# One program for two attentions and two feed-forward layers: stages joined without barriers

## The reference

```
x = x + attention_a(layernorm(x))    # 16 heads of 8, causal; heads 0 to 2 up-weight a third of the tokens
x = x + ffn(layernorm(x))
x = x + attention_b(layernorm(x))    # 16 heads of 8, rotary embedding of q and k, no mask
x = x + ffn(layernorm(x))            # the same ffn weights

ffn(x): h = silu(lin1(x)) * lin2(x)  # 128 to 512, ternary weights times a scale per output
        h = gelu(h1(h)); h = gelu(h2(h))   # 512 to 512, exact gelu
        return lin3(h)                     # 512 to 128
```

## Time and profile before

| | |
|---|---|
| time, median of 3 runs | 2213.65 us (2210.31 to 2215.91) |
| the profiled execution: time | 2211.82 us |
| its span, first to last instruction | 2210.1 us |
| mean granted clock of TensorE | 0.947 |
| busy: PE, DVE, ACT, POOL | 1950.2 (88%), 1722.8 (78%), 1476.5 (67%), 1093.7 us (49%) |

### The profile page before, as it was taken

How to read it: one execution, slowest core, us unless ns; L and a number is a source line. 1 busy time by engine, 2 the same in 40 slices (tenths; PEclk the granted TensorE clock), 3 DMA queues, 4 the chain that set the end, 5 groups by cost and what they waited for, 6 DMA issues and landing times. The chain is left out here.

```text
span 2210.1 us, 43095 instructions
## 1 busy us (share of the span) xinstructions
PE 1950.2 (88%) x16198; PEld 991.0 (45%) x16198; DVE 1722.8 (78%) x2358; ACT 1476.5 (67%) x2633; POOL 1093.7 (49%) x1550
## 2 busy tenths in 40 slices
PE   3889989998849999993799999999999976999998
PEld 1333333343337778771122222222222224777776
DVE  4878878888448888851899999999998916888883
ACT  1567767777726666660288888888888973666665
POOL 6777777776415555554233343342433002555555
PEclk9999999999969999996599999999999997999999
DMA  7556555654100000004333444334444110000000
GB/s 171 105 114 130 114 115 122 122 116 104 23 12 1 1 1 1 1 1 99 71 66 70 89 89 96 73 70 96 89 92 85 32 19 5 10 15 10 15 14 16
DMA packets 106212, 136.72 MB, mean 62 GB/s; under 512 B 21008, under 2 KB 89872, under 8 KB 99856
## 3 DMA queue, kind: packets, MB, share of 16 engines
q1 hardware_dynamic: 106000, 133.89, 28.9%
HBM read 67.78 MB, written 55.57 MB: 56 GB/s over the span
## 5 line engine op out<-in xcount | busy, mean ns | idle before, releaser
L709 DVE TENSOR_REDUCE b_negmax<-ps_max 128x2 f32<-128x1024 f32 x512 | 593.2, 1217 | 54.5 <-PE ps_max L848 53.7
L814 ACT ACTIVATE b_prob<-ps_score 128x512 f32<-128x512 f32 x1024 | 552.3, 596 | 97.4 <-PE ps_score L830 88.2
L814 ACT ACTIVATE a_prob<-ps_score 128x512 f32<-128x512 f32 x640 | 346.4, 599 | 91.6 <-PE ps_score L830 83.0
L709 DVE TENSOR_REDUCE a_negmax<-ps_max 128x2 f32<-128x256 f32 (+2 forms) x384 | 314.3, 863 | 84.2 <-PE ps_max L865 79.0
L886 PE MATMUL ps_out<-b_prob,b_v_aug 128*9 128x256 f32 x4096 | 316.8, 382 | 21.7 <-ACT b_o_raw L779 20.9
L609 POOL TENSOR_SCALAR_AFFINE_SELECT a_prob<-a_prob 128x256 f32<-128x256 f32 (+1 forms) x448 | 188.1, 439 | 147.0 <-ACT a_prob L814 146.5
L1143 PE MATMUL ps_score<-fa_h,w_hi 128*128 128x512 f32 x1024 | 247.6, 396 | 0.7 <-ACT fa_h2f L1086 0.4
L1143 PE MATMUL ps_score<-fb_h,w_hi 128*128 128x512 f32 x1024 | 247.5, 396 | 0.7 <-ACT fb_h2f L1086 0.4
L848 PE MATMUL ps_max<-stack_k,b_stack_q 48*128 48x512 bf16 x1024 | 214.2, 394 | 29.9 <-DVE b_negmax L709 14.3
L830 PE MATMUL ps_score<-b_stack_q,stack_k 50*128 50x512 bf16 x1024 | 219.3, 389 | 12.7 <-DMA b_stack_q<-b_nm_rows 7.5
L1143 PEld LDWEIGHTS ps_score<-fa_h,w_hi 128*128 128x128 f32 x1024 | 191.8, 189 | 45.7 <-ACT fa_h2f L1086 0.9
(11 more groups left out here) (155 smaller groups left out, 3194.2 us busy)
## 6 DMA issues: line engine op xcount, KB each, us to landing
stack_k<-d_stack SPq DMA_DIRECT2D x64, 384.0 KB, 6.2
d_stack<-a_parts SPq DMA_DIRECT2D x64, 192.0 KB, 2.8
a_stack_q<-d_stack SPq DMA_DIRECT2D x32, 384.0 KB, 5.6
d_stack<-b_parts SPq DMA_DIRECT2D x64, 192.0 KB, 2.8
b_stack_q<-d_stack SPq DMA_DIRECT2D x32, 384.0 KB, 5.6
d_stack<-a_parts SPq DMA_DIRECT2D x64, 128.0 KB, 2.8
d_stack<-b_parts SPq DMA_DIRECT2D x64, 128.0 KB, 2.8
x<-in_x SPq DMA_DIRECT2D x16, 256.0 KB, 6.7
```

The costliest lines, as they stand in the source:

```text
L709: last = dve.tensor_reduce(m["negmax"][:, t, :, p], banks[:, :, at:at + w], AX.X, ALU.max, negate=True)
L814: act.activation(prob(b, i)[:, o], act_bank("score", 2 * i + o), ACT.Exp).then_inc(s["prob"], 1)
```

## The change

All stages stand in one block with one set of buffers (`buffers`; the attention's and the FFN's large ones overlap in SBUF) and one barrier at the end. Each engine runs attention a's steps -1 to 16, then a joint routine for the attention's steps 17 to 19 and the FFN, then attention b from step 1 or 2, and again the joint routine.
- In the joint routine the norm and transposes of FFN batch 0 lie in step 17, its gates behind step 17 and between the blocks of step 18; the output products of batches 14 and 15 lie behind the gates and in the FFN's batch 0, in bank `ps_out`.
- In the last two batches of the first FFN (r = 14 and 15) the rotary attention's batches 0 and 1 are prepared: norms, transposes, q, qr, k, kr, v in bank `ps_misc`, parts, stores and loads, and step 1 with the maxima of batch 0.
- The flag of the weights is made in steps 8 to 10 of the causal attention, with two small DMAs in place of a transpose. PE reads it after step 17 and branches there, once for each FFN; the attention's drain and the rotary preparation stand inside both branches.
- The rotary attention's weights load during the first FFN. Some semaphores are merged (`moments`; `var` and `neg_mean` share one).

```diff
...
+        first = attention(nc, sem, m, a, "a", True, f)
+        second = attention(nc, sem, m, a, "b", False, f)
+        ffn = feed_forward(nc, m, a, out, f)
+        with nc.Block() as block:
+            @block.sync
+            def _(sp):
+                first.parts["sync_begin"](sp, None)
+                for n in range(-1, B + 3):
+                    first.sync(sp, n)
+                second.parts["sync_begin"](sp, first)
+                second.parts["sync_fill"](sp)
+                for n in range(1, B + 3):
+                    second.sync(sp, n)
+                ffn.sync(sp)
...
+            @block.tensor
+            def _(pe):
+                for n in range(-1, B + 1):
+                    first.tensor(pe, n)
+                ffn.tensor(pe, 0, first, second)
+                for n in range(2, B + 1):
+                    second.tensor(pe, n)
+                ffn.tensor(pe, 1, second, None)
+        nc.all_engine_barrier()
+        nc.clear_and_free_semaphores(own)
+        nc.all_engine_barrier()
...
+    EARLY = {"q": 2, "qr": 2, "k": 2, "kr": 2, "v": 1} if rotary else {}
+    LOOP_END = B + 2
...
+        if rotary and i == 0 and b == 1:
+            sp.wait_ge(f["h1"], count(FT, B))
...
+    def sync_fill(sp):
+        store(sp, 0, "stored_q", 0)
+        load(sp, 0, "stack_q", "stored_q", 0)
+        store(sp, 0, "stored_k", 1)
+        load(sp, 0, "stack_k", "stored_k", 1)
+        store(sp, 1, "stored_q", 0)
...
+        if causal and n == FLAG_STEP:
+            sp.wait_ge(f["halved"], 3)
+            sp.dma_start(m["d_flags"].rearrange("(p o) -> p o", o=1), m["flags"][:]).then_inc(f["flag_moved"], 16)
+        if causal and n == FLAG_STEP + 1:
+            sp.wait_ge(f["flag_moved"], 16)
+            sp.dma_start(m["flag_row"][:], m["d_flags"].rearrange("(o p) -> o p", o=1)).then_inc(f["flag_moved"], 16)
...
+    def pool_fill(pool):
+        high(pool, 1, "q", 0)
+        middle_low(pool, 1, 0)
+        add_bias(pool, 0)
+        pool.wait_ge(f["h3_hi"], count(FT, B))
+        ones(pool, range(1, VALUES))
+        norm(pool, 2)
+        negated_max_parts(pool, 0, 0)
+        high(pool, 1, "k", 1)
+        middle_low(pool, 1, 1)
+        add_bias(pool, 1)
+        high(pool, 2, "q", 0)
+        middle_low(pool, 2, 0)
...
+    def pool_layer(pool, l, before, after):
+        first, left = B * l, before.parts
+        norm_rstd(pool, m, s, first)
+        before.pool(pool, B + 1, 0, 6)
+        norm_rstd(pool, m, s, first + 1)
+        before.pool(pool, B + 1, 6)
+        left["weighted"](pool, B - 2)
+        for r in range(B):
+            b = first + r
+            if r + 2 < B:
+                norm_rstd(pool, m, s, b + 2)
+            if after is None or r < B - 2:
+                low(pool, b, 2, range(FT))
+                if r == 0:
+                    left["weighted"](pool, B - 1)
+                low(pool, b, 3, range(FT))
+                if after is not None and r == B - 3:
+                    after.parts["ones"](pool, (0,))
+                    after.parts["widen_bias"](pool)
+                    after.parts["norm"](pool, 0)
+                continue
+            fill = after.parts
+            if r == B - 2:
+                low(pool, b, 2, range(FT))
+                fill["high"](pool, 0, "q", 0)
+                low(pool, b, 3, range(0, 2))
+                fill["middle_low"](pool, 0, 0)
+                low(pool, b, 3, range(2, 4))
+                fill["high"](pool, 0, "k", 1)
+                fill["middle_low"](pool, 0, 1)
+            if r == B - 1:
+                low(pool, b, 2, range(FT))
+                fill["norm"](pool, 1)
+                low(pool, b, 3, range(FT))
+                fill["pool_fill"](pool)
...
+        normed(first)
+        norm_stats(dve, m, s, first + 1, (before.s["resid"], 2))
+        before.vector(dve, B + 1)
+        xT_low(dve, first)
+        norm_apply(dve, m, s, first + 1)
+        for r in range(-1, B - 1):
+            b = first + r
+            gated(dve, b + 1, 0)
+            gated(dve, b + 1, 1)
+            if after is not None and r == B - 2:
+                after.parts["project"](dve, 0, "q", 0)
+                after.parts["turn"](dve, 0, "q", 0)
+            if r == -1:
+                dve.wait_ge(before.s["pv"], count(before.plan.blocks, B))
+            if 0 <= r < B - 2:
+                normed(b + 2)
+            split(dve, b + 1, 0)
+            split(dve, b + 1, 1)
+            if r == -1:
+                left["invert"](dve, B - 1)
+                left["residual"](dve, B - 2)
+            if r == 0:
+                left["residual"](dve, B - 1)
+            if r > 0:
+                add_y(dve, b - 1)
+            gated(dve, b + 1, 2)
+            split(dve, b + 1, 2)
...
+        after.vector(dve, 1, 0, 8)
+        fill["project"](dve, 1, "q", 0)
+        after.vector(dve, 1, 8, 10)
+        fill["turn"](dve, 1, "q", 0)
+        after.vector(dve, 1, 10, 12)
+        add_y(dve, first + B - 1)
+        after.vector(dve, 1, 12, 14)
+        fill["project"](dve, 1, "k", 1)
+        after.vector(dve, 1, 14, 16)
+        fill["turn"](dve, 1, "k", 1)
+        after.vector(dve, 1, 16)
...
+        if l == 0:
+            act.wait_ge(s["halved"], 2)
+        before.scalar(act, B + 1, 0, 12)
+        xT_high(act, first)
+        before.scalar(act, B + 1, 12)
+        gate(act, first, 0)
+        gate(act, first, 1)
+        before.scalar(act, B + 2)
...
+    def tensor_both(pe, l, before, after):
+        first = B * l
+        before.tensor(pe, B + 1, 0, 10)
+        pe.wait_ge(before.s["max"], count(before.plan.beats, B))
+        transposes(pe, first)
+        before.tensor(pe, B + 1, 10)
+        pe.wait_ge(s["halved"], 5)
+        has_low = pe.value_load(m["flag"][:], min_val=0, max_val=1)
+        with pe.If(has_low):
+            tensor_layer(pe, l, before, after, True)
+        with pe.Else():
+            tensor_layer(pe, l, before, after, False)
...
+        pe.wait_ge(over["resid"], B - 2)
+        gates(first, 0)
+        gates(first, 1)
+        before.tensor(pe, B + 2)
+        gates(first, 2)
+        gates(first, 3)
+        pe.wait_ge(over["prob"], count(2 * before.plan.beats, B))
+        transposes(pe, first + 1)
+        left["output_product"](pe, B + 2, B - 2)
+        gates(first + 1, 0)
+        gates(first + 1, 1)
+        for r in range(B):
+            b = first + r
+            fill = after.parts if after is not None else None
+            layer(b, 2, (0,))
+            if fill and r == B - 2:
+                fill["turn_x"](pe, -1, 0)
+            layer(b, 2, (1,))
+            if fill and r == B - 2:
+                fill["fill_linear"](pe, 0, "q")
+            layer(b, 2, (2,))
+            if fill and r == B - 2:
+                fill["fill_linear"](pe, 0, "qr")
+            layer(b, 2, (3,))
+            if fill and r == B - 2:
+                fill["fill_linear"](pe, 0, "k")
+            if r > 0:
+                turn_y(pe, b - 1)
+            if r + 1 < B:
+                gates(b + 1, 2)
+            if r == 0:
+                left["output_product"](pe, B + 3, B - 1)
+            if fill and r == B - 2:
+                fill["fill_linear"](pe, 0, "kr")
+            if fill and r == B - 1:
+                after.tensor(pe, 1, 0, 2)
+                layer(b, 3, (0, 1), lambda: after.tensor(pe, 1, 2, 4))
+                after.tensor(pe, 1, 4, 6)
+                fill["turn_x"](pe, 0, 1)
             else:
...
+                layer(b, 3, (0, 1))
+            if r + 1 < B:
+                gates(b + 1, 3)
+            if r + 2 < B:
+                transposes(pe, b + 2)
+            if fill and r == B - 2:
+                fill["fill_linear"](pe, 0, "v")
+            layer(b, 3, (2,))
+            if fill and r == B - 2:
+                fill["bias_product"](pe, m["ps_misc"][:, 0:D])
+            if fill and r == B - 1:
+                after.tensor(pe, 1, 6, 8)
+            layer(b, 3, (3,))
+            if fill and r == B - 1:
+                fill["fill_linear"](pe, 1, "q")
+                after.tensor(pe, 1, 8, 10)
+            if r + 2 < B:
+                gates(b + 2, 0)
+                gates(b + 2, 1)
+            if r == 0:
+                pe.wait_ge(over["resid"], B)
+            wait(pe, s["resid"], b)
+            for i in range(FT):
+                pe.wait_ge(s["h3"], count(FT, b, i + 1))
+                at = W_AT["out"] + D * i
+                mm = product(m["ps_out"][:], slice(at, at + D), lambda part: h[3][:, part, i], i == 0, i == FT - 1)
+            mm.then_inc(s["yT_ps"], 1)
+        if after is not None:
+            fill["fill_linear"](pe, 1, "qr")
+            after.tensor(pe, 1, 10, 12)
+        turn_y(pe, first + B - 1)
+        if after is not None:
+            after.tensor(pe, 1, 12, 13)
+            fill["fill_linear"](pe, 1, "k")
+            after.tensor(pe, 1, 13, 16)
+            fill["fill_linear"](pe, 1, "kr")
+            after.tensor(pe, 1, 16)
```

(2 more changed lines are left out.)

1603 lines of the change are left out of this document (822 added, 781 removed).

## The result

The changed kernel takes 2160.8 us (median of four runs, 2157.8 to 2165.5) where the kernel before, beside it, took 2213.7 (2210.3 to 2215.9): ratio 0.9764, 95% interval 0.9742 to 0.9786, that is 52.9 us less. The profiled execution has a time of 2165.5 us and a span of 2163.4. That is 46.7 us less span than before, against 64.3 in the sum.

A forecast was written before the change was run, and what follows sets the result against it. One engine is full inside the stages but none between them, so the time lies in three seams: 20.9 + 23.8 + 20.6 - 1 = 64.3 us off 2211.8 gives 2147.5, median level 2149.3, stated as 2150; range 2132 to 2166.

The forecast's parts named there:

- batch 15's product: In each FFN's batch 0, PE stands at batch 15's output product, waiting for POOL's oT: 4.1 us given back.
- Seam 1: Causal attention's end into the first FFN: layer 2 starts 25.0 us earlier, less 4.1 given back, so 20.9 us gained.
- wait at the reciprocal: DVE stands for the reciprocal's DMA before h1's second half: 3 us at the causal attention's end, 1 at the rotary's.
- the wait for the parts: In step 17, POOL's norm_rstd work delays the last negated maxima's parts: 1.5 us causal, 3.5 us rotary.
- the jump: PE's flag reading and branch into its conditional part, no longer hidden behind the norm: 2 us, from 0 to 4.5.
- Seam 2: First FFN into rotary attention, batches 0 and 1 prepared early: batch 1's maxima 23.8 us earlier, 10 to 35.
- the stand at kr: In the first FFN's batch 14, PE waits for DVE to take k out of the shared bank: 6.3 us.
- Seam 3: Rotary attention's end into the second FFN: layer 2 starts 24.7 us earlier, less 4.1 given back, so 20.6 us gained.
- its new waits at step 8 and 9 stand ahead of a load used a step later: SP's new waits in the causal attention, for the flag's small DMAs, were claimed to cost nothing.
- rival D: DVE and POOL slow each other in the FFN, 2.6 us longer per batch: 83 us lost, 2232; chance 0.05.
- B: Better case: jump and product's stall hidden, maxima's delay absorbed; 92 us gained, 2121; chance 0.12.
- rival A: Rotary preparation collides with the FFN's tail and both drains stand longer: 42 us gained, 2171; chance 0.16.

## Why the prediction was right, and where not

The time fell inside the range, 11 us above the value, for the mechanism named: the seams close, the stages stay. Its signs of being right came (batch 14 36.1 us long, PE 9.4 us behind the load of stack_k, 3.7 and 3.6 us at batch 15's product), and so did one of its signs of being wrong: the rotary step 17 grew by 7.3 us, over its 6. By its steps:

- **Seam 1** right in sum: 20.9 forecast, 26.5 - 0.4 - 6.0 = 20.1 measured. Its parts erred both ways, so that it came out this close is partly luck: the fill from the gates took 17.7 us, not 19.6 (less of a wait at the reciprocal, 0.65 instead of 3), the wait for the parts cost 0.4 with all else in step 17, not 1.5 and 0.6, the jump 4.0 instead of 2, batch 15's product 6.0 instead of 4.1.
- **Seam 2** right, 23.8 forecast, 25.9 by the traces and 26.8 by undoing it. Batch 14 took 36.1 us (35.6 forecast), parts to first maximum 13.0 (12.9), from there to batch 1 57.2 (59.5). Its account of the stand at kr was right in size (5.9 for 6.3) and in lying on the path: moved, it gave 4.6 us up to the first maximum. What it left out is the slow layer 3 behind it, 2.1 us.
- **Seam 3** wrong in size: 20.6 forecast, 23.3 - 7.3 - 7.8 = 8.2 measured. The late parts were seen (4.4 for 3.5), the jump and the product too. The failed step is the term behind each: what PE does after such a stand was priced at the high clock. What it cost: 2.3 us in step 17; in the fill, 21.4 us from gates to layer 2 instead of 17.6 (16.3 without a jump), of which 1.4 is the second gap; 3.1 of the 7.8 in batch 0, by what filling the stand gave back. The jump itself took 1.7 us more than forecast. The earlier trace rows had shown the clock of 0.50 to 0.61 in the seams, and the text quoted it, but only one term used it, the longer wait at seam 1's reciprocal, and that wait didn't come about.
- **"its new waits at step 8 and 9 stand ahead of a load used a step later"**, priced at nothing, was wrong by 6.6 us. The wait for the flag did cost nothing. The transfer ahead of it did, by what it does to stores in flight.
- **The rest** held: steady batches as they were, rival D's slowing of VectorE by GpSimd didn't come about in the FFN (21.7 us a batch before and after), B's hidden product and jump neither. What happened is the forecast with the heavier terms of rival A: not the collision in the fill, but the stands.

## What to carry to other kernels

Price a stand of TensorE of about 4 us twice, itself and the slow work that mostly follows it (here 1.5 to 3.7 us), and prefer filling it with any work over leaving it. A branch that used to lie in idle time costs some 4 us once it is on the path, before what it does to the clock; put it where the engine stands anyway, and only once. When an edit adds a transfer, ask what is in flight beside it, not only who waits for it; and when it makes an engine wait, follow who feeds the queues of the others.
